# Four mixed layers on one core: the receptance weights ahead of the value weights in the ring of three

## The reference, cut to what matters

```python
xxx = jnp.tanh((xa + sx * maa_x) @ maa_w1).reshape(b, l, 5, DM)
xxx = jnp.einsum('blfd,fde->blfe', xxx, maa_w2)
xm = xa[:, :, None] + sx[:, :, None] * (maa_stack + xxx)
xk, xw, xv, xr, xg = (xm[:, :, j] for j in range(5))
w = jnp.exp(-jnp.exp(time_decay + jnp.tanh(xw @ td_w1) @ td_w2)).reshape(b, l, h, s_)
r = (xr @ Wr.T).reshape(b, l, h, s_)
k = (xk @ Wk.T).reshape(b, l, h, s_)
v = (xv @ Wv.T).reshape(b, l, h, s_)
g = jax.nn.silu(xg @ Wg.T)
# recurrence over the tokens, per head:  a = k v^T;  out = r (u*a + s);  s = a + w*s
x1 = x + og * g @ Wo.T          # og: out, normalised per head
# then a feed-forward part with Wfk, Wfr and Wfv
```

## Time and profile before

| what | us |
|---|---|
| median of 3 runs (lowest, highest) | 4369.45 (4360.58, 4370.68) |
| the profiled execution, whole | 4371.74 |
| its span | 4369.8 |
| PE busy | 3802.8 (87%) |
| DVE busy | 2631.0 (60%) |
| ACT busy | 2290.0 (52%) |
| POOL busy | 1688.0 (39%) |

### The profile page before, as it was taken

The page is one execution under the profiler, slowest core; times in us unless marked ns, Lnnn a source line. Parts: engine busy times, 40 slices in busy tenths (PEclk is TensorE's granted clock), DMA queues, the critical chain, the costliest instruction groups (busy, mean ns, idle before and its releaser), DMA issues. The chain is left out here.

```text
span 4369.8 us, 65250 instructions
## 1 busy us (share of the span) xinstructions
PE 3802.8 (87%) x23680; PEld 2348.6 (54%) x23680; DVE 2631.0 (60%) x5803; ACT 2290.0 (52%) x4528; POOL 1688.0 (39%) x1869
## 2 busy tenths in 40 slices
PE   7889899888888989988888998898888888889897
PEld 4444555555544455555654545555565444655555
DVE  5765646656576564565657656466566775546655
ACT  5665734434566563443466756344346575634444
POOL 4544542222454454222245445422224644542222
PEclk9999999998899999989989999998989999999898
DMA  4032210102203221010220322101022132210102
GB/s 132 15 118 63 73 67 30 58 20 97 72 16 117 63 73 67 30 58 20 97 73 25 107 63 82 58 30 58 20 97 76 40 90 69 76 58 30 58 30 97
DMA packets 94554, 276.01 MB, mean 63 GB/s; under 512 B 25472, under 2 KB 25984, under 8 KB 73088
## 3 DMA queue, kind: packets, MB, share of 16 engines
q1 hardware_dynamic: 94208, 271.58, 19.3%
HBM read 201.24 MB, written 4.19 MB: 47 GB/s over the span
## 5 line engine op out<-in xcount | busy, mean ns | idle before, releaser
L806 POOL TENSOR_SCALAR probs<-probs,row_inv 128x512 f32<-128x512 f32 x1024 | 693.1, 693 | 641.0 <-DVE row_inv L721 641.0
L665 ACT ACTIVATE probs<-probs,row_max 128x512 f32<-128x512 f32 x1024 | 733.4, 725 | 131.8 <-DVE row_max L737 130.4
L560 PE MATMUL ps<-ident,probs 128*128 128x128 f32 x4096 | 610.3, 290 | 176.8 <-ACT pT L659 150.9
L560 PEld LDWEIGHTS ps<-ident,probs 128*128 128x128 f32 x4096 | 480.6, 147 | 386.3 <-ACT pT L659 215.6
L370 PE MATMUL ps<-mix,wring 128*128 128x512 f32 x1024 | 485.3, 612 | 36.4 <-DMA wring<-in_blocks_dram 36.4
L659 ACT ACTIVATE pT<-ps 128x512 f32<-128x512 f32 x768 | 431.0, 602 | 113.7 <-PE ps L560 113.3
L535 PE MATMUL ps<-kstack,qstack 96*128 96x512 f32 (+1 forms) x1024 | 378.3, 464 | 16.4 <-DMA qstack<-hi 7.3
L737 DVE CUSTOM_DVE_ANT_0 probs<-ps,maskA 128x512 f32<-128x512 f32 x512 | 329.4, 681 | 43.3 <-PE ps L535 43.3
L737 DVE CUSTOM_DVE_ANT_0 probs<-ps,neg 128x512 f32<-128x512 f32 x512 | 340.6, 685 | 8.8
L370 PEld LDWEIGHTS ps<-mix,wring 128*128 128x128 f32 x1024 | 196.4, 195 | 235.7 <-issue 188.5
L1550 POOL TENSOR_TENSOR hinv<-hvar,minus_half 128x32 f32<-128x32 f32 x24 | 146.2, 6093 | 289.4 <-DVE hvar L1260 289.4
(11 more groups left out here) (179 smaller groups left out, 7339.8 us busy)
## 6 DMA issues: line engine op xcount, KB each, us to landing
wring<-in_blocks_dram SPq DMA_DIRECT2D x151, 1024.0 KB, 5.2
qstack<-hi SPq DMA_DIRECT2D x256, 64.0 KB, 2.0
kstack<-hi SPq DMA_DIRECT2D x256, 64.0 KB, 2.0
maskA<-in_mask_dram SPq DMA_DIRECT2D x9, 1024.0 KB, 7.6
rows<-in_rows_dram SPq DMA_DIRECT2D x8, 1024.0 KB, 4.6
qstack<-hi SPq DMA_DIRECT2D x256, 32.0 KB, 2.0
qstack<-lo SPq DMA_DIRECT2D x128, 64.0 KB, 2.0
kstack<-lo SPq DMA_DIRECT2D x128, 64.0 KB, 2.0
```

Source lines behind the costliest of these rows:

```text
L560: ins = nc.tensor.transpose(tile[:, qc * P:(qc + 1) * P], probs[:, m % PSLOTS, qc, kc * P:(kc + 1) * P], ident[:, :])
L665: nc.scalar.activation(p, p, ACT.Exp, bias=row_max[:, n % PSLOTS, qc:qc + 1], scale=-1.0, accum_out=row_sum[:, n % PSLOTS, qc:qc + 1]).the ...
L806: nc.gpsimd.tensor_scalar(p, p, row_inv[:, (n - 1) % PSLOTS, qc:qc + 1], 1.0, ALU.mult, ALU.mult)\
```

## The change

In the order of the ring, the receptance weights and the value weights of both recurrent layers change places. The code of every engine stays as it is. The places of r and v follow from the numbers: r is now number 21 (30 in layer 3) in place 0, and v number 22 (31) in place 1.

```diff
 for _layer in (2, 3):
-    BLOCKS += [f'{n}_{_layer}' for n in ('small', 'k', 'v', 'r', 'g', 'o', 'fk', 'fr', 'fv')]
+    BLOCKS += [f'{n}_{_layer}' for n in ('small', 'k', 'r', 'v', 'g', 'o', 'fk', 'fr', 'fv')]
```

## The result

The changed kernel took 4308.07 us (median of 4 runs, 4298.77 to 4313.14) against 4366.3 us before (four runs now, where the table before had three with a median of 4369.45); the ratio is 0.9863, with a 95% interval of 0.985 to 0.9876. That is 58 us less (54 to 65). The forecast was 4310.

A forecast was written before the change was run, and what follows sets the result against it. PE, busy 87% of the span, was taken as the bound. Gains of 51.4 us (receptance and values), 4.5 (waits for o) and 4.7 (clock there) sum to 60.6, giving 4310 us; range 4298 to 4322, or to 4336 including a rival.

The forecast's parts named there:

- The wait for r: PE's idle time before the receptance projection, 4.55 us on average, would go in all eight places.
- G: Start of PE's first mixing product of g, from which the stage up to the start of L915 is timed.
- The place of the values: Value weights land at G + 5.05, leaving 0.58 us of wait; L915 starts at G + 9.34, gaining 51.4 us in eight places.
- The clock as a share of it: From G to L915, 18.4 us of the gain is low clock and 33.0 us is idle time removed.
- Block o: Issued some 9 us earlier in head group 2; 4.5 us of ACT's waits and 4.7 us of slow running would go.
- The clock is lost elsewhere: Rival: clock falls come at other PE waits instead; gain only 37.5 us, 4332 from the median; chance 0.20.
- The gain is waited off: Rival: another engine, DVE with its pair products, holds PE up in head group 0; about 4365 us; chance 0.06.
- The slower rival: Values land late on the path of L915; at 15.7 us in all places, 53 us lost, 4422 us; chance 0.03.

The follow-up runs named there:

- fill_before: Kernel before the change, plus five full-width products of no use behind the first mixing product of g, filling the stall for r; 4328.4 us, ratio 0.9903.
- v_late: Changed kernel, but the value weights are issued only when the last mixing product of g is done; 4350.4 us, ratio 0.9965.
- o_late: Changed kernel, but block o's load waits for the last use of v too, as before the change; 4317.9 us, ratio 0.9884.
- o_late_five: Changed kernel with block o's load waiting for v's last use too, repeated in five rounds; 4325.0 us, ratio 0.9906.
- pad_after: Changed kernel plus five products of no use, 16 columns each, behind the first mixing product of g; 4288.7 us, ratio 0.9809.

## Why the prediction was right

**The wait for r.** Forecast: gone in eight of eight, with r's load early enough. So it was; the first receptance chunk follows G by 0.34 us in all eight, and the others at full pace, 1.09 us apart.

**The place of the values.** Forecast: G + 5.05, with 0.58 us of waiting and L915 at G + 9.34. Measured: 0.39 us of waiting on average and 75.3 / 8 = 9.41 us. The forecast gain of 51.4 us came out as 50.8. The range of the forecast also counts 4.4 us more for a faster load, and no run shows such a load: the loads of the values took 4.65 to 5.19 us to land (up to 5.47 in the two further profiles), and a wait remained in all eight places.

**The clock as a share of it.** Forecast: 18.4 us of low clock (0.50 behind the stall), apart from 33.0 us of idle time. `fill_before` took away the former alone and measured 17.3. That the remaining wait (0.16 to 0.98 us) leaves the clock alone was right in all 24 places of three profiles. It isn't so everywhere: in front of L1006, waits of 0.59 to 0.86 us were followed by low clock in seven places of the two kernels with o late, and waits of 0.64 to 0.81 us in three others weren't. The mean clock rose as forecast, from 0.942 to 0.950 to 0.955.

**Block o.** Forecast: 4.5 us of waits and 4.7 us of clock, 9.2 us in total. The waits went, all of them, and head group 3 became 9.7 us shorter. In the kernel before it had 5.5 us of waits at L1006 and 10.2 us at 0.50, of which half is 5.1. Counting the clock was right, and both sizes were close; putting o back cost 10.7 and 12.5 us.

**The total.** The two parts were forecast at 51.4 and 9.2 us and measured at 50.8 and 9.7, in rows that repeat. That the median after is within 2 us of 4310 is luck beyond that: the three medians of the changed kernel are 4306.0 to 4311.3, and that of the kernel before moved from 4369.45 to 4366.3 with one more run.

**Rivals.** "The clock is lost elsewhere" fell. The 58.0 us at 0.50 between G and L915 went to none, and outside that stretch the low clock went down too, from 447.8 us to 386.9, 434.5 and 421.3. From L915 to wo it was 34.1 us before and 13.7, 30.7 and 27.3 after. These last three are one kernel in three executions. "The gain is waited off" fell with DVE's idle time at L1222 and with head groups 0 to 2, which took 715.9 to 726.5 us against 720.0. The slower rival's price was about right: in `v_late` the values were issued at G + 3.86 and landed 4.79 us later on average, for which its sum gives 15.25 us a place, and 14.84 was measured. Its condition didn't occur, as the values were never waited for longer than 1.0 us.

What is left open: the 7.9 us in work that the change doesn't touch came with one profile and went with the next two. `o_late` and `fill_before` had them as well (2719.0 and 2718.8 us), `o_late_five` and `v_late` not (2723.6 and 2726.0), so they don't belong to an edit, and I have no cause for them.

## What to carry to other kernels

In a ring of buffers, the order of the loads can differ from the order in which blocks seem to belong together: give the place that frees last to the block that is needed last, and check which release each block behind it inherits, since here a sixth of the gain (9.7 us) came from a block that no line of the change names. Price a stall of the matrix engine with the low clock behind it (17.3 of the 50.8 us here), and measure that part by filling the stall with products of no use. To credit a gain to an edit, look for the stretch that the edit touches and that repeats from profile to profile: block o's 9.7 us stood out in head group 3, and were blurred in the stretch around it. And look whether the edit moved instructions: ten more matmul records in each recurrent layer were worth some 20 us here.

## What the runs showed of the hardware

**Idle time of PE without a releaser.** In the kernel before, PE stopped for 1.5 to 2.2 us in L972 in 7 of 8 layers with no releaser in the profile, at the same product each time, in layer 2 in head group 1 and in layer 3 in head group 2. Behind six of the seven the clock was at 0.50 for 3.4 us or more, and the products there ran slow as well. These rows are PE's timeline of the kernel before, sample 0, layer 2:

```profile
695.29 1.78 PE L972 MATMUL ps<-v_blocks,k_tok 32*32 32x128 f32 x115
698.60 0.44 PE L972 MATMUL ps<-v_blocks,k_tok 32*32 32x128 f32 x13 [1.53 <-issue]
698.97 3.01 PE L930 MATMUL ps<-rk,head_sum 128*128 128x512 f32 x4
```

L930 takes 1.98 us at full clock. L972's products follow each other closest of all in the kernel, 128 in 1.9 us. In `pad_after` and in `fill_before`, ten records stand ahead of this place, and the wait comes ten products earlier. So in `pad_after`:

```profile
685.34 1.68 PE L975 MATMUL ps<-v_blocks,k_tok 32*32 32x128 f32 x105
688.66 0.71 PE L975 MATMUL ps<-v_blocks,k_tok 32*32 32x128 f32 x23 [1.65 <-issue]
```

It belongs to a place in PE's list and not to a product: all 36 waits in layer 2, over the ten profiles, are at the 3160th matmul record of the pass. In layer 3 all 24 waits are at the 5169th, in the seven profiles without added products. In the three with them, where layer 3 is shifted by 20 or 55 records, the wait was absent in all twelve places, though a product of L972 stood at the 5169th record there too; for this I have no explanation. What such a wait costs is seen where it is absent by chance. With o early, L915 to wo took 119.71, 119.80 and 119.96 us in the three such places of the profiles without added products, and 120.98 to 125.19 us, with a median of 123.5, in the 29 where PE had waited: about 1.8 us of idle time, and for most of the rest low clock, 3.4 or 6.8 us at 0.50 in 22 of the 29. No run here shows what PE waits for in that time.

**Low clock without idle time.** In `pad_after` PE ran ten matmul records of 16 columns (1.27 us in the place shown) behind full work, and the clock was at 0.50 behind them for 3.4 us in three of eight places, all in layer 3, with no idle time of PE. In `fill_before`, where the ten had 512 columns, it stayed at 1.00 in all eight.
